# Second FFN of one more chunk held back to the end, and two held-back FFN tiles split around TensorE transposes

## What is computed

```
x = x + 0.5 * ffn(layernorm(x))
x = x + attn(layernorm(x))
x = x + 0.5 * ffn(layernorm(x))

ffn(t):  t and weight are rounded in blocks of 32 to a 6-bit grid times a scale (absmax / 7.5)
         return td @ wd.T + bias
attn(t): q, k, v = t @ Wq, t @ Wk, t @ Wv            (8 heads of 128)
         ret = ((q k^T / sqrt(128)) * decay) v       (causal, decay per head)
         ret = (ret - mean) * rsqrt(var + 1e-6)      (per row and head)
         return (silu(t @ W_G) * ret) @ W_O
```

## Time and profile before

| | |
|---|---|
| device time, 3 runs | 487.41, 487.58, 566.6 us, median 487.58 us |
| profiled execution | 486.2 us |
| span of its slowest core (core 2) | 484.4 us |
| spans of the 8 cores | 481.7 to 484.4 us |
| TensorE busy | 431.2 us, 89% of the span |
| VectorE busy | 343.6 us, 71% |
| GpSimd busy | 256.5 us, 53% |
| ScalarE busy | 190.6 us, 39% |

### The profile page before, as it was taken

The page is one execution under the profiler, slowest core; times in us unless marked ns, Lnnn a source line. Parts: engine busy times, 40 slices in busy tenths (PEclk is TensorE's granted clock), DMA queues, the critical chain, the costliest instruction groups (busy, mean ns, idle before and its releaser), DMA issues.

```text
span 484.4 us, 8182 instructions; the slowest of 8 cores (481.7 to 484.4 us)
## 1 busy us (share of the span) xinstructions
PE 431.2 (89%) x2410; PEld 215.6 (45%) x2456; DVE 343.6 (71%) x656; ACT 190.6 (39%) x270; POOL 256.5 (53%) x328
## 2 busy tenths in 40 slices
PE   0225799999998799999999999999999999999894
PEld 0113354545543445454544545454545454555442
DVE  3887867477788859688686868586947566756782
ACT  1547365244441161607062433416151534614400
POOL 0888776135486464654647455647451624436243
PEclk9999999999999899999999999999999999999998
DMA  7999999975354383644453533635340524233143
GB/s 197 316 178 188 186 159 186 155 102 113 74 105 83 91 183 96 99 77 132 78 140 65 153 67 87 89 87 88 85 79 13 109 45 85 47 66 65 44 153 131
DMA packets 99451, 54.47 MB, mean 112 GB/s; under 512 B 88784, under 2 KB 89040, under 8 KB 99408
## 3 DMA queue, kind: packets, MB, share of 16 engines
q1 hardware_dynamic: 93984, 43.43, 39.5%
q0 software_dynamic: 5280, 10.49, 14.4%
q10 hardware_dynamic: 144, 0.03, 0.0%
HBM read 34.28 MB, written 8.39 MB: 88 GB/s over the span
## 4 chain that ended last, share of the span: by engine, by line
PE 76%; DVE 12%; issue 7%; ACT 2%; DMA 1%; POOL 1%; DVEq 1%; ACTq 0%; POOLq 0%
PE p L815 68%; DVE p L419 2%; DVE arena L444 2%; DVE arena L434 1%; PE p L925 1%; PE p L856 1%; PE pstate L905 1%; PE p L844 1%; PE pstate L869 1%; DMA arena<-wf 1%; PE p L860 1%; ACT arena L706 1%; DVE arena L449 1%; DVE arena L522 1%; DVE arena L447 1%
## 5 line engine op out<-in xcount | busy, mean ns | idle before, releaser
L815 PE MATMUL p<-arena 128*128 128x512 bf16 x1715 | 383.2, 379 | 5.3 <-ACT arena L706 2.7
L815 PEld LDWEIGHTS p<-arena 128*128 128x128 bf16 x1760 | 170.2, 98 | 203.2 <-issue 6.6
L434 DVE BATCH_NORM_STATS2 arena<-arena 128x6 f32<-128x512 f32 x96 | 66.4, 692 | 10.1 <-DVE arena L436 2.4
L666 ACT ACTIVATE arena<-arena 128x1024 bf16<-128x1024 f32 x16 | 19.9, 1243 | 132.9 <-POOL arena L1069 132.9
L1109 POOL TENSOR_TENSOR arena<-arena 128x1024 bf16<-128x1024 fp8e4 x16 | 34.3, 2143 | 46.0 <-DVE arena L449 46.0
L678 ACT ACTIVATE arena<-p,arena 128x128 bf16<-128x128 f32 x128 | 46.4, 472 | 19.2 <-POOL arena L1082 19.2
L513 DVE TENSOR_TENSOR arena<-p,arena 128x1024 bf16<-128x1024 f32 x16 | 19.6, 1222 | 43.2 <-PE p L815 42.9
L444 DVE TENSOR_REDUCE arena<-arena 128x32 f32<-128x1024 f32 x29 | 35.3, 1216 | 16.5 <-ACT arena L657 10.5
L905 PE MATMUL pstate<-arena 128*128 128x128 bf16 x168 | 15.4, 251 | 35.2 <-POOL arena L1045 27.7
L1102 POOL TENSOR_TENSOR arena<-arena 128x1024 bf16<-128x1024 fp8e4 x16 | 30.6, 1910 | 27.8 <-DVE arena L449 27.8
L449 DVE SCALAR_TENSOR_TENSOR arena<-arena 128x1024 fp8e4<-128x1024 f32 x29 | 38.8, 1337 | 3.4 <-DVE arena L448 0.5
(11 more groups left out here) (52 smaller groups left out, 397.7 us busy)
## 6 DMA issues: line engine op xcount, KB each, us to landing
arena<-x SPq DMA_DIRECT2D x16, 512.0 KB, 6.0
out<-arena SPq DMA_DIRECT2D x16, 512.0 KB, 2.8
arena<-wf SPq DMA_DIRECT2D x8, 512.0 KB, 11.3
arena<-wk POOLq DMA_DIRECT2D x2, 1024.0 KB, 20.2
arena<-wq POOLq DMA_DIRECT2D x2, 1024.0 KB, 30.7
arena<-wg POOLq DMA_DIRECT2D x2, 1024.0 KB, 39.1
arena<-wv POOLq DMA_DIRECT2D x2, 1024.0 KB, 40.2
arena<-wo POOLq DMA_DIRECT2D x2, 1024.0 KB, 33.4
```

The lines of the kernel that those rows point to most:

```text
L434: step(e.bn_stats(bn_ln[:, n, 6 * half:6 * half + 6], x[:, 512 * half:512 * half + 512]))
L815: last = e.matmul(pair[:, half * 512:half * 512 + 512], lhs[:, kc, :], w[:, kc, half * 512:half * 512 + 512], start=(kc == 0), stop=(kc == ...
```

## The change

`F2_IN` goes from 9 to 8: `f2(8)` leaves iteration i = 11 of the loop and becomes the first tile of the tail, so eight second FFNs are held back rather than seven. Iteration 11 takes the order that iteration 12 has (`wo` ahead of `ret`, `evO` ahead of `gn`), and the list of PSUM users follows. The transposed input of `f2(8)` gets a home in the first `xd1_sb` buffer, for which `xdt2(8)` on SP waits until the DMA transpose of `xd1(14)` is done.

In the tail `f2(11)` and `f2(14)` are cut into column halves (`f2_half`). The first half of `f2(11)` stands between `turn z15` and `wo(15)`, the second behind `wo(15)`; the first half of `f2(14)` stands ahead of `turn y15`, the second behind it. VectorE's tail is `mask(15)`, `gn(15)`, `ev2(8)`, `evO(14)`, `st3(14)`, `ev2(9)`, `zmul(15)`, `ev2(10)`, `q2(14)`, and from `ev2(11)` on as before.

```diff
-F2_IN = 9
+F2_IN = 8
@@ psum_users
-        if i == LATE - 1:
+        if F2_IN + 3 <= i < LATE:
             order += [("f1", i + 3, 0), ("sc", i - 1, 1), ("wo", i - 2, 2),
@@
-    order += [("sc", 15, 1), ("f2", 9, 2), ("ret", 15, 1), ("wo", 14, 0), ("f2", 10, 2),
-              ("f2", 11, 0), ("wo", 15, 1), ("f2", 12, 2), ("f2", 13, 0), ("f2", 14, 2),
-              ("f2", 15, 1)]
+    order += [("sc", 15, 1), ("f2", 8, 2), ("ret", 15, 1), ("wo", 14, 0), ("f2", 9, 2),
+              ("f2", 10, 0), ("f2", 11, 2), ("wo", 15, 1), ("f2", 12, 0), ("f2", 13, 2),
+              ("f2", 14, 0), ("f2", 15, 1)]
@@ xdt2 on SP
+            elif c == 8:
+                e.wait_ge(sem["tr_x10"], 16 * n_dma(14, X1_DMA, 2))
@@ tail of prog_vector
         mask(NC - 1)
-        ev2(9)
         gn(NC - 1)
+        ev2(8)
         evO(NC - 2)
         st3(NC - 2)
+        ev2(9)
+        zmul(NC - 1)
         ev2(10)
-        zmul(NC - 1)
         q2(NC - 2)
         ev2(11)
         evO(NC - 1)
@@ prog_tensor
+        def f2_half(c, half):
+            e.wait_ge(sem["tr_x2"], 16 * (c + 1))
+            pair = emptied("f2", c)
+            for kc in range(KC):
+                last = e.matmul(pair[:, half * 512:half * 512 + 512], xdt2_at(c)[:, kc, :],
+                                wdt_sb[:, kc, half * 512:half * 512 + 512],
+                                start=(kc == 0), stop=(kc == KC - 1),
+                                skip_group_check=True)
+            if half == 1:
+                last.then_inc(sem["t_f2"], 1)
@@ tail of prog_tensor
         sc(NC - 1)
-        f2(9)
+        f2(8)
         ret(NC - 1)
         wo(NC - 2)
+        f2(9)
         f2(10)
-        f2(11)
         e.wait_ge(sem["s_Sc"], NC - 1)
         e.wait_ge(sem["v_z"], NC)
         turn("z%d" % Z_PE, z_sb)
+
+        f2_half(11, 0)
         wo(NC - 1)
+        f2_half(11, 1)
         f2(12)
         f2(13)
-        f2(14)
+        f2_half(14, 0)
         e.wait_ge(sem["g_xd2"], NC)
         turn("y%d" % X2_PE, xd2_sb)
+        f2_half(14, 1)
         f2(NC - 1)
```

More of the change, by code:

```diff
@@ L180, in build_program @@
     y82_sb = f8at(take(1024), D)
-    xd1_sb = [bfat(take(2048), D) for _ in range(2)]
+    o_xd1 = [take(2048) for _ in range(2)]
+    xd1_sb = [bfat(o, D) for o in o_xd1]
     o_xd2 = take(2048)
@@ L242, in build_program @@
     wd_sb = [bfat(o_v, D), bfat(o_st, D)]
-    late_home = {9: cols(o_xc1[0]), 10: cols(o_xc1[0] + 2048), 11: cols(o_xc1[1]),
+    late_home = {8: cols(o_xd1[0]), 9: cols(o_xc1[0]), 10: cols(o_xc1[0] + 2048), 11: cols(o_xc1[1]),
                  12: cols(o_xc1[1] + 2048), 13: xdt1_sb[0], 14: xdt1_sb[1]}
@@ L397, in prog_sync @@
                 xdt1(i + 5)
+        store(8)
         store(9)
@@ L598, in prog_vector @@
                 st2(i + 1)
-            if i >= LATE - 1:
+            if i >= F2_IN + 3:
                 evO(i - 2)
@@ L603, in prog_vector @@
             gn(i - 1)
-            if i >= LATE - 1:
+            if i >= F2_IN + 3:
                 st3(i - 2)
-            if i < LATE - 1:
+            else:
                 evO(i - 2)
@@ L1181, in prog_gpsimd @@
             smG(i - 1)
-            if i >= LATE - 1:
-                sm3(i - 2)
-            if i < LATE - 1:
-                sm3(i - 2)
+            sm3(i - 2)
             if i + 5 < NC:
```

## The result

| | before | changed |
|---|---|---|
| median of the first runs | 487.5 us | 492.12 us (493.5, 491.99, 491.08, 492.24) |
| ratio to before, 95% interval | | 1.009 [1.0064, 1.0115] |
| median, measured again (6 runs) | 487.21 us | 490.0 us (489.8 to 492.14), 1.0068 [1.0054, 1.0082] |
| and a third time (6 runs) | 487.08 us | 489.93 us (489.25 to 491.63), 1.0063 [1.0046, 1.0079] |
| profiled execution, span on the slowest core | 484.4 us | 491.7 us |

The change makes the kernel slower by about 0.6 to 0.9%, which is under 2%. The first median, 492.1 us, is 2.0 us above the forecast of 490.1 and 0.3 us above the top of the range, 491.8. The two later medians of the same kernel, 490.0 and 489.9, are at the forecast. So two things are to be explained: the 2.8 us that every measurement has in common, and why four runs could come out another 2 us higher.

A forecast was written before the change was run, and what follows sets the result against it. TensorE, busy 431.2 of 484.4 us, was taken as the bound. Terms -3.45 + 0.6 + 3.9 + 1.5 = +2.55 us put the median at 490.1 us; own range 489.2 to 491.2, 8-in-10 range 486.9 to 491.8.

The forecast's parts named there:

- Part 1: Loop: f2(8) leaving iteration 11 saves 3.45 us; v(11) waits a new 0.6 us for evQ(11).
- Rival (c): Loop: the wait at v(11) makes later iterations late too, twice more 0.6 us; 491.3 us; chance 0.07.
- Part 2: Tail's first stall: f2(9) waits 0.6 us for ev2(8), which moved behind gn(15).
- Part 3: Tail: the halves cover ScalarE's two copies behind the turns, removing a wait of 1.35 us at each place.
- Part 4: Tail: evO(15) queues behind ev2(11) on VectorE; turn y15 waits 3.2 us, f2(15) starts 3.9 us later, including Part 2.
- Rival (b): Tail: VectorE does not hold up evO(15), and no wait at v(11); -2.45 us, 485.1 us; chance 0.13.
- Part 5: Tail: TensorE's clock falls to 1.2 GHz behind turn y15, costing 1.5 us (bounds 0 and 1.7).
- Rival (a): Tail: the clock holds behind turn y15, so +1.05 us, 488.6 us; chance 0.17.

The follow-up runs named there:

- e3_evq: Changed kernel with ScalarE doing evQ(i) ahead of norm(i-1) from iteration 11 on: 489.66 us against 487.55 before, ratio 1.0056.
- e1_evo_first: Changed kernel with VectorE's evO(15) and st3(15) ahead of ev2(11), and q2(15) ahead of ev2(12): 486.82 us against 487.21 before, ratio 0.9998.
- e6_all: Changed kernel with the edits of e1_evo_first and e3_evq, ev2(8) ahead of gn(15), PSUM pairs of f2(14) and f2(15) exchanged: 484.9 us against 487.21 before.
- e2_filler: Changed kernel with twelve matmuls, result unread, filling the wait ahead of turn y15: 488.69 us against 487.21 before, ratio 1.0032.

## Why the prediction was right in its steps and too low in its top

**Part 1, the loop.** Right. Forecast -3.45 + 0.6 = -2.85 us and 23.1 from `sc(10)` to `sc(11)`; measured -2.81 and 23.15 to 23.17, so the 0.63 us of lateness at `mask` passed through VectorE and ScalarE to `evQ(11)` whole. Not foreseen: 0.34 us more at `v(12)`. Rival (c) named a wait in later iterations, at 0.6 us and twice; it was about half of that, and once. What I had written against it, that from iteration 12 on the order is that of before, left out that the earlier trace rows show no slack there either: TensorE came to `v(12)` just as `evQ(12)` ended, so any lateness had to show. But this lateness isn't that of `v(11)` carried on, as (c) had it: `mask(11)` starts 0.78 us after `sc(11)`, as before. It comes in on VectorE ahead of `evO(10)`; core 2 before, then changed:

```profile
371.34 1.23 DVE L484 TENSOR_TENSOR arena<-p,arena 128x1024 f32<-128x1024 f32 x1 [0.24 <-DVE arena L436]
```

```profile
373.51 1.23 DVE L489 TENSOR_TENSOR arena<-p,arena 128x1024 f32<-128x1024 f32 x1 [0.59 <-DVE arena L441]
```

`e3_evq` has the same 0.59 us there, without a wait at `v(11)`. What holds up `evO(10)` is open.

**Part 2, the first stall of the tail.** Right: forecast 0.6 us, measured 0.64 (printed as 0.47).

**Part 3, the copies.** Right: both waits of 1.35 us are gone.

**Part 4, VectorE's queue.** Right: `evO(15)` 3.2 us after `wo(15)` (forecast 3.2), behind `ev2(11)`; 3.19 us of wait at `turn y15` (forecast 3.2). `e1_evo_first` shows that this is the cause. Rival (b), 485.1 us, falls as the change was written. `e6_all` comes near its number with 484.9 us, but mends the waits at `v(11)`, `v(12)` and `f2(9)` as well.

**Part 5, the clock on an ordinary core.** Right: taken at 1.5 us, measured 1.5 by `e2_filler`. The bound of 1.7 was exceeded only as told below. Rival (a) took the chance that it holds. Of 24 cores in the three profiled executions of the changed kernel it held on two up to the last matmul; 20 lost 1.3 to 1.7 us, counted from the granted clock of the 9 us behind `turn y15`. With a slowest core to be taken from eight, a hold here and there can't help.

**The sum.** Forecast +2.55: -2.85 in the loop, +3.9 + 1.5 = +5.4 in the tail. Measured -2.81, +0.34 and +5.4, together +2.8 to 2.9, which is the forecast and the wait at `v(12)`. Two of three medians agree: 490.0 and 489.9 against 490.1.

**What failed: the step from the change's own terms to the slowest of eight cores, and two sizes.** I took the rest of the kernel as fixed and added only the change's terms to the median of before; what lies ahead of `sc(10)` stood in the sum at nothing, and I gave no reason. But the start-up has a spread of its own, on cores that are drawn anew at each execution, and the slowest core is one on which start-up and tail add up badly. Take the profiled execution: 491.7 - 484.4 = 7.3 us are 4.6 before `sc(10)` on core 2 and 2.7 from there on. The next slowest, core 5 at 488.4, gives with the 1.8 us around the span 490.2.

The second is the upper bound of part 5. I wrote "Lower bound 0, upper 1.7" from the 3.4 us at the lower clock in the earlier trace rows. Two of 24 cores stayed down for about 6 us and lost 3.0 (core 3 above is one). The trace of before had such a case, which I didn't read: on core 1 the granted clock is 0.60 from 53 to 57 us and 0.55 from 57 to 61, after waits of 1.40 and 1.35 us. It also speaks against my sentence that waits of 1.35 us cost no core its clock. Of the profiled execution's 491.7 us this bound explains nothing, since core 2 lost 1.5 us behind `turn y15`. The third is the 0.34 us at `v(12)`.

The range itself was added up wrongly. With the clock at 1.7 for 1.5 and `v(11)` at 1.0 for 0.6, its own upper end is 490.1 + 0.2 + 0.4 = 490.7 us, not 491.2; with 3.0 for the clock it would be 492.0, and the first median still lies above.

The other three first runs, 491.1 to 492.2, have as slowest cores ones with a mean clock of 0.984 to 0.986, lower than the 0.988 of core 5. In the twelve repeats that was so in three (492.14, 490.39 and 490.79 us). Of the other nine one took 491.63 with 0.989, for which I have no trace, and eight took 489.3 to 490.1, seven of them at 0.987 or 0.988.

**What stays open.** Sixteen runs of the changed kernel were timed, and the first four are all among the six highest. If all sixteen were alike, chance would do that in less than 1 case of 100, so something of the chip or the hour is likely in it; what, no run shows, since the first four were not made beside the repeats. So the 2 us by which the first median exceeds the later ones are accounted for in one execution only. What delayed the other three is read from their clocks alone. The fall of the clock between 48 and 57 us came on 8 of 24 cores in kernels with `F2_IN = 9` and on 28 of 64 with `F2_IN = 8` and no matmuls added in the start-up. Three more of the 24 had one at 45 to 47 us, which cost nothing from the first matmul to `sc(0)`; with them it is 11 of 24. Either way the difference is within chance.

## What to carry to other kernels

When a tile is split around another to cover a copy, its eviction moves too. On an engine that works in order, put the eviction that the last chain hangs on ahead of the split tile's, and then look at which PSUM buffer waits next: here the first step took the measure from +2.8 to -0.9 us against before, and the buffers with two more reorderings took it to -3.15, with the same matmuls. A wait of 3 us on TensorE near the end cost its own length here and then again half of the slow stretch behind it (1.5 us on most cores); if the wait can't be removed, matmuls that nobody reads may fill it. On eight cores, read a term on all of them and set the range by the worst, and add the spread of the stages that the change doesn't touch.
